# Two fused layers on one core: causal masks added by VectorE inside the maximum, and a unit's last product issued in the next unit

## The reference, cut to what matters

```python
def _causal_attn(q, k, v):
    scale = 1.0 / math.sqrt(q.shape[-1])
    scores = jnp.einsum('bthd,bshd->bhts', q, k) * scale
    t = q.shape[1]
    mask = jnp.tril(jnp.ones((t, t), dtype=bool))
    scores = jnp.where(mask, scores, -jnp.inf)
    attn = jax.nn.softmax(scores, axis=-1)
    return jnp.einsum('bhts,bshd->bthd', attn, v)
...
ctx = _causal_attn(q, k, v)                      # 16 heads of 16 features
conv_out = jax.lax.conv_general_dilated(ctx_c, conv_w, window_strides=(1,), padding=[(1, 1)], ...) + conv_b
q2 = conv_out.transpose(0, 2, 1).reshape(b, s, NUM_HEADS, HEAD_DIM)
ctx2 = _causal_attn(q2, k, v)
out = ctx2.reshape(b, s, d) @ out_w.T + out_b
```

## Time and profile before

| | us |
|---|---|
| median of 3 runs | 2189.26 |
| lowest, highest | 2182.49, 2190.48 |
| the profiled execution, its own time | 2200.97 |
| its span, first to last instruction | 2199.1 |
| last stage (turns 0 to 31 of the second layer), from 1237.7 | 961.4 |
| TensorE busy in the span | 1917.2 (87%) |
| VectorE busy | 1284.2 (58%) |
| ScalarE busy | 905.3 (41%) |
| granted TensorE clock, mean | 0.94 |

### The profile page before, as it was taken

How to read it: one execution, slowest core, us unless ns; L and a number is a source line. 1 busy time by engine, 2 the same in 40 slices (tenths; PEclk the granted TensorE clock), 3 DMA queues, 4 the chain that set the end, 5 groups by cost and what they waited for, 6 DMA issues and landing times.

```text
span 2199.1 us, 32188 instructions
## 1 busy us (share of the span) xinstructions
PE 1917.2 (87%) x11791; PEld 941.1 (43%) x11801; DVE 1284.2 (58%) x2839; ACT 905.3 (41%) x1633; POOL 403.0 (18%) x651
## 2 busy tenths in 40 slices
PE   4888988899858999996589798999999999999987
PEld 2222322323212666664234344545445454545444
DVE  5888778777852333332553665666565656565653
ACT  0354555455533111111244344445444445444444
POOL 3232333123151111111442100000010100000000
PEclk8789989989977999998699899999999999999999
DMA  4445444532413111112104235354543444443440
GB/s 110 102 106 117 110 94 99 95 57 56 87 40 133 32 32 34 30 34 91 38 20 86 45 69 80 60 90 84 83 86 64 87 73 82 81 91 62 73 69 21
DMA packets 131217, 159.55 MB, mean 73 GB/s; under 512 B 22419, under 2 KB 115731, under 8 KB 129014
## 3 DMA queue, kind: packets, MB, share of 16 engines
q1 hardware_dynamic: 126630, 148.18, 34.3%
q0 software_dynamic: 4432, 9.33, 1.5%
HBM read 111.26 MB, written 46.19 MB: 72 GB/s over the span
## 4 chain that ended last, share of the span: by engine, by line
PE 65%; DVE 13%; DMA 7%; ACT 5%; issue 3%; POOL 2%; SPq 2%; another core or an unknown queue 1%; DVEq 0%; POOLq 0%
PE p_PV L659 11%; PE p_S L619 8%; PE p_S L643 8%; PE p_PV L739 6%; DVE t_mx L994 6%; PE p_S L715 5%; PE p_Ma L835 4%; PE p_Ma L589 4%; DMA msd<-t_msp 3%; SPq L1699 2%; PE p_S L646 2%; PE p_S L622 2%; PE p_S L728 2%; PE p_Ma L597 2%; ACT t_spl L1370 2%
## 5 line engine op out<-in xcount | busy, mean ns | idle before, releaser
L1387 ACT ACTIVATE t_R<-p_S 128x512 f32<-128x512 f32 (+1 forms) x1216 | 668.5, 574 | 628.5 <-PE p_S L646 332.6
L994 DVE TENSOR_REDUCE t_mx<-p_S 128x1 f32<-128x512 f32 (+3 forms) x1216 | 750.0, 656 | 219.5 <-PE p_S L622 139.5
L619 PE MATMUL p_S<-t_R 96*128 96x512 bf16 (+3 forms) x1536 | 488.2, 346 | 51.5 <-DVE t_mx L994 31.1
L643 PE MATMUL p_S<-t_R 99*128 99x512 bf16 (+3 forms) x1536 | 487.5, 341 | 43.7 <-ACT t_R L1387 16.6
L659 PE MATMUL p_PV<-t_R 128*17 128x512 f32 (+3 forms) x3072 | 338.4, 514 | 1.7 <-ACT t_R L1387 1.4
L619 PEld LDWEIGHTS p_S<-t_R 96*128 96x128 bf16 x1536 | 151.3, 100 | 397.5 <-DVE t_mx L994 236.9
L643 PEld LDWEIGHTS p_S<-t_R 99*128 99x128 bf16 x1536 | 152.6, 100 | 225.9 <-ACT t_R L1387 96.0
L1588 POOL CAST t_spl<-t_rr 128x512 bf16<-128x512 f32 x80 | 48.9, 611 | 953.3 <-DVE t_rr L958 953.3
L622 PE MATMUL p_S<-t_maskq,t_identb 128*128 128x128 bf16 x1024 | 200.6, 223 | 0.0
L646 PE MATMUL p_S<-t_maskk,t_identb 128*128 128x128 bf16 x1024 | 198.9, 220 | 0.0
L1224 DVE TENSOR_SCALAR t_spl<-p_S,t_B1T 128x128 f32<-128x128 f32 x312 | 84.4, 343 | 135.8 <-PE p_S L728 135.3
(11 more groups left out here) (204 smaller groups left out, 1905.3 us busy)
## 6 DMA issues: line engine op xcount, KB each, us to landing
t_R<-qs SPq DMA_DIRECT2D x288, 128.0 KB, 4.3
t_R<-ks SPq DMA_DIRECT2D x288, 128.0 KB, 4.9
qs<-t_spl SPq DMA_DIRECT2D x48, 384.0 KB, 2.3
t_R<-in_w SPq DMA_DIRECT2D x16, 1024.0 KB, 5.3
ks<-t_spl SPq DMA_DIRECT2D x32, 384.0 KB, 5.7
ysd<-t_cT SPq DMA_DIRECT2D x39, 128.0 KB, 1.7
t_X<-in_x SPq DMA_DIRECT2D x8, 512.0 KB, 3.6
h0d<-t_cT SPq DMA_DIRECT2D x8, 512.0 KB, 2.9
```

The lines of the kernel that those rows point to most:

```text
L619: t = self.nc.tensor.matmul(bank[:, z, :], qa[0:96, h, qb * 128:(qb + 1) * 128], ka[0:96, h, 0:n], start=True, stop=not u.causal)
L643: t = self.nc.tensor.matmul(bank[:, z, :], ka[0:99, h, kb * 128:(kb + 1) * 128], qa[0:99, h, n0:512], start=True, stop=not u.causal)
L994: nc.vector.tensor_reduce(m.mx[:, g, i:i + 4 * len(js) - 3:4], m.S1[k % 3][:, 0:len(js) * n].rearrange("p (j n) -> p j n", j=len(js)), AX. ...
L1387: nc.scalar.activation(m.P[p % 2][:, j0:j0 + per, 0:n], m.s2_bank(k)[:, 0:per * n].rearrange("p (j n) -> p j n", j=per), ACT.Exp, scale=0. ...
```

## The change

1. In `maxp` the mask matmul goes. VectorE's `tensor_reduce` over one to four slices in a bank becomes, for a causal unit, one `tensor_tensor_reduce` for each slice: it adds `maskq`, now 512 columns wide with zeros ahead of the triangle, writes the sum back into the bank, and gives the maximum of the row.
2. The masks are filled with -2^127 by GpSimd at once; VectorE's two multiplications and the semaphore `masks` go.
3. In `expp` a causal unit's last product stays in `self.late` and is issued after the second score step of the next unit, with its `close` behind it (`finish`). A turn still has 26 steps of `expp`.
4. So that the product has its input kept, the exponentials of causal units go into four buffers `P1`, one for each kb; ScalarE waits for the product four back, not two.
5. `pre1` of a kind 2 unit with c = 0 starts four of its steps later (LATE2, steps 8, 10, 12 of the turn in place of 0, 2, 4), `fin1` three of its own (LATE: 9, 12, 15, 18 in place of 0, 3, 6, 9), on all engines.

```diff
 def pre1(self, u):
-        return steps(3 if u.kind == 1 else 2 if u.c else 4)
+        return steps(3 if u.kind == 1 else 2 if u.c else LATE2 + 4)
...
     def expp(self, u):
-        late = None
         for g in range(2):
             for kb in range(4):
...
                     self.scores(u, g, kb, j0, per, n0)
-                    if late is not None and j0 + per >= 2:
-                        self.product(u, *late)
-                        done, late = late, None
-                        if done[1] == 3:
-                            yield
-                            yield from self.close(u, done[0])
+                    if self.late is not None and j0 + per >= 2:
+                        yield from self.finish()
                     yield
-                late = (g, kb)
-        self.product(u, *late)
-        yield
-        yield from self.close(u, 1)
+                self.late = (u, g, kb)
+        if not u.causal or u.n == 47:
+            yield from self.finish()
+
+    def finish(self):
+        (u, g, kb), self.late = self.late, None
+        self.product(u, g, kb)
+        if kb == 3:
+            yield
+            yield from self.close(u, g)
...
 TensorE.maxp
-                                              start=True, stop=not u.causal)
-                    if u.causal:
-                        t = self.nc.tensor.matmul(bank[:, z, n - 128:n], m.identb[:, :], m.maskq[:, :],
-                                                  start=False, stop=True)
+                                              start=True, stop=True)
...
 TensorE.product
-                                      m.P[p % 2][:, j, 0:512 - n0], start=(kb == 0), stop=(kb == 3),
+                                      m.P1[kb][j] if u.causal else m.P[p % 2][:, j, :], start=(kb == 0), stop=(kb == 3),
...
 VectorE.maxp
-                nc.vector.tensor_reduce(
-                    m.mx[:, g, i:i + 4 * len(js) - 3:4],
-                    m.S1[k % 3][:, 0:len(js) * n].rearrange("p (j n) -> p j n", j=len(js)),
-                    AX.X, ALU.max).then_inc(s.s1_read, 1)
+                if u.causal:
+                    e.wait_ge(s.consts, 6)
+                    for z in range(len(js)):
+                        sc = m.S1[k % 3][:, z * n:z * n + n]
+                        x = nc.vector.tensor_tensor_reduce(
+                            out=sc, in0=sc, in1=m.maskq[:, 512 - n:512],
+                            scale=1.0, scalar=NEG, op0=ALU.add, op1=ALU.max,
+                            accum_out=m.mx[:, g, i + 4 * z:i + 4 * z + 1])
+                    x.then_inc(s.s1_read, 1)
+                else:
+                    nc.vector.tensor_reduce(m.mx[:, g, i:i + 1], m.S1[k % 3][:, :], AX.X, ALU.max).then_inc(s.s1_read, 1)
...
 ScalarE.scores
-        if p >= 2:
+        if u.causal and p >= 132:
+            e.wait_ge(s.pv_mm, p - 3)
+        elif u.causal:
+            e.wait_ge(s.x2_base, NB)
+            e.wait_ge(s.p_mm, NB)
+        elif p >= 2:
             e.wait_ge(s.pv_mm, p - 1)
...
 pre1, kind 2, c = 0: TensorE and ScalarE
+            yield from steps(LATE2)
 VectorE, GpSimd and SyncE
-            yield
-            yield
+            yield from steps(LATE2 + 2)
...
 GpSimd.begin
-        g.affine_select(out=m.maskq[:, :], in_=m.maskq[:, :], compare_op=ALU.is_ge, fill=1.0,
-                        **down).then_inc(s.consts, 1)
+        g.affine_select(out=m.maskq[:, 384:512], in_=m.maskq[:, 384:512], compare_op=ALU.is_ge, fill=NEG,
+                        **down).then_inc(s.consts, 1)
```

More of the change, by code:

```diff
@@ L18 @@
 NEG = -(2.0 ** 127)
+LATE2 = 4
+LATE = 3
 QP, KP = (0, 0, 0, 1, 1, 2), (0, 1, 2, 0, 1, 0)
@@ L365, in __init__ @@
         self.c2T = self.xTb
+        self.P1 = [[R2[:, 12288 + 512 * j:12800 + 512 * j] for j in range(4)],
+                   [R2[:, 14336 + 384 * j:14720 + 384 * j] for j in range(4)],
+                   [(R2[:, 15872:16384], R3[:, 512:1024])[j // 2][:, 256 * (j % 2):256 * (j % 2) + 256] for j in range(4)],
+                   [R3[:, 1024 + 128 * j:1152 + 128 * j] for j in range(4)]]
+        self.P1X = [[p.rearrange("p (j n) -> p j n", j=1) for p in self.P1[0]],
+                    [p.rearrange("p (j n) -> p j n", j=1) for p in self.P1[1]],
+                    [R2[:, 15872:16384].rearrange("p (j n) -> p j n", j=2),
+                     R3[:, 512:1024].rearrange("p (j n) -> p j n", j=2)],
+                    [R3[:, 1024:1536].rearrange("p (j n) -> p j n", j=4)]]
     def v_tile(self, u):
@@ L382, in __init__ @@
         self.consts = sem("consts")
-        self.masks = sem("masks")
         self.ones3 = sem("ones3")
@@ L451, in __init__ @@
         self.raw = engine
+        self.late = None
         self.begin()
@@ L507, in pre1 @@
     def pre1(self, u):
-        return steps(3 if u.kind == 1 else 2 if u.c else 4)
+        return steps(3 if u.kind == 1 else 2 if u.c else LATE2 + 4)
     def fin1(self, u):
-        return steps(4) if u.kind == 2 and u.c else none()
+        return steps(LATE + 4) if u.kind == 2 and u.c else none()
     def expp(self, u):
-        late = None
         for g in range(2):
@@ L607, in maxp @@
         e.wait_ge(s.d_f[1][u.buf], 96 * u.fill)
-        if u.causal:
-            e.wait_ge(s.masks, 2)
         for g in range(2):
@@ L849, in fin1 @@
         e, m, s, b = self.e, self.m, self.s, u.b
+        yield from steps(LATE)
         for c in range(2):
@@ L1332, in fin1 @@
         nc, e, m, s, b = self.nc, self.e, self.m, self.s, u.b
-        yield
-        yield
+        yield from steps(LATE + 2)
         for h in range(2):
@@ L1384, in scores @@
         e.wait_ge(s.s2_mm, k + 1)
-        if p >= 2:
+        if u.causal and p >= 132:
[4 more added lines that the diff above has]
+        elif p >= 2:
             e.wait_ge(s.pv_mm, p - 1)
         nc.scalar.activation(
-            m.P[p % 2][:, j0:j0 + per, 0:n], m.s2_bank(k)[:, 0:per * n].rearrange("p (j n) -> p j n", j=per),
+            m.P1X[kb][j0 // per] if u.causal else m.P[p % 2][:, j0:j0 + per, :],
+            m.s2_bank(k)[:, 0:per * n].rearrange("p (j n) -> p j n", j=per),
             ACT.Exp, scale=0.25 if u.causal else 1.0).then_inc(s.s2_exp, 1)
@@ L1502, in begin @@
         down = dict(base=0, pattern=[[-1, 128]], channel_multiplier=1)
-        for t in (m.ident, m.identb, m.maskq, m.maskk):
+        for t in (m.ident, m.maskq, m.identb, m.maskk):
             g.memset(t[:, :], 0.0).then_inc(s.consts, 1)
@@ L1507, in begin @@
                         **down).then_inc(s.consts, 1)
+        g.affine_select(out=m.maskq[:, 384:512], in_=m.maskq[:, 384:512], compare_op=ALU.is_ge, fill=NEG,
+                        **down).then_inc(s.consts, 1)
         g.affine_select(out=m.identb[:, :], in_=m.identb[:, :], compare_op=ALU.not_equal, fill=1.0,
                         **down).then_inc(s.consts, 1)
-        g.affine_select(out=m.maskq[:, :], in_=m.maskq[:, :], compare_op=ALU.is_ge, fill=1.0,
-                        **down).then_inc(s.consts, 1)
-        g.affine_select(out=m.maskk[:, :], in_=m.maskk[:, :], compare_op=ALU.is_ge, fill=1.0, base=0,
+        g.affine_select(out=m.maskk[:, :], in_=m.maskk[:, :], compare_op=ALU.is_ge, fill=NEG, base=0,
                         pattern=[[1, 128]], channel_multiplier=-1).then_inc(s.consts, 1)
@@ L1830, in fin1 @@
         e, m, s, b = self.e, self.m, self.s, u.b
-        yield from steps(4)
+        yield from steps(LATE + 4)
         e.wait_ge(s.out_add, 2 * b + 2)
```

8 lines of the change are left out of this document (2 added, 6 removed).

## The result

The changed kernel takes 2200.96 us in the median of 13 runs (2192.94 to 2208.95); the kernel before took 2185.68 beside it (13 runs, 2179.79 to 2192.97). The ratio is 1.0070, 95% interval 1.0054 to 1.0087: 15 us slower. Forecast were 2208 us, 18.5 over the median of the kernel before. The execution profiled after has a span of 2199.7 us and took 2201.47, near its median; the one of before was 15 us over its own, and lost them between the two attention stages, in code that the change does not touch: the preparation of the second layer's first unit starts at 1048 us there, at 1035 in the changed kernel.

What follows compares the result with a forecast made beforehand. With three banks PE can't run ahead, so VectorE's chain was followed, with late transfers stalling convolution turns. -19.6 + 0 + 15.6 + 9.9 + 13.6 - 1 = +18.5 us on the median 2189.3: 2208 us, range 2150 to 2250.

Steps and rivals of the forecast that it cites:

- the place of the loss: Six convolution turns with output projection: later convolution delays q's write and twelve transfers, each turn 2.6 us longer, +15.6 us.
- Turns 2 and 28: Convolution turns without the output projection: transfers land at 36.4 us, turns 5.3 and 4.6 us longer, +9.9 us.
- the turns with a second convolution: Eight turns (3, 7, ..., 27, 29): 28.3 us forecast, 28.3 in the mean measured before, so 0 change.
- the clock: Eight stalls of over 4 us before PE-heavy convolutions lower the granted clock: 8 x 1.7 = +13.6 us.
- projection turns: Fourteen turns (0, 1, 4, 5, ..., 24, 25): 27.3 us each, 1.4 less, -19.6 us in all.
- A group is then ... 8.78 us, 1.76 more: VectorE's maxima for four heads: 16 instructions, 8.78 us against 7.02 before, 3.5 us more a turn.
- I follow VectorE's chain: Projection turns: PE can't run ahead with three banks, so VectorE's chain sets the turn: 26.8 us, 27.3 with 0.4 added.
- PE has 2.7 us less a turn: PE's queue: 1.86 us a turn from removed mask matmuls and 0.80 from no wait before the last product's transpositions.
- The transfers land in time: Rival: quicker fill or earlier step 12, by 4.6 us together, so no turn stalls: -36 us, 2153 us; chance 0.2.
- The read costs nothing, the stall stays: Rival: the maximum's read is free, 1.3 us off 22 turns, -29 us: net -10, 2179 us; chance 0.17.
- The new maximum is dearer: Rival: its read takes a whole instruction, 2.1 us on 22 turns and 0.8 on eight, +52 us: 2260; chance 0.13.
- PE is the bound and all of its gain is kept: Rival: all 32 turns get 2.7 us shorter, -86 us: 2103 us; chance 0.05.

Runs made afterwards that it cites:

- E2: The kernel before with only the late product, its buffers and the shifts, masks still by matmuls and one maximum a bank: 2217.64 us, ratio 1.0158.
- E4: The changed kernel with SyncE issuing the six transfers of k at the start of the turn, ahead of those of q: 2151.5 us, ratio 0.9858.
- E8: The changed kernel with k's transfers first and the convolution at step 2 instead of 4, last output a step sooner: 2146.7 us, ratio 0.9791.
- E7: The changed kernel with the 1024 mask matmuls put back, adding zeros: 2221.25 us, ratio 1.0156.
- E10: E8 with every causal maximum reading only 128 columns and the exponential's scale 2 to the -14: 2117.5 us, ratio 0.9715.
- E6: E2 (late product alone, masks by matmul) with the transfers of KA issued first: 2168.7 us, ratio 0.9914.
- E9: E8 with the 1024 matmuls put back, adding zeros: 2174.95 us, ratio 0.9962.
- E5: The kernel before with one edit, the transfers that fill KA issued first: 2171.9 us, ratio 0.9915.

## Why the prediction was right, and where its steps were not

**Right: the place of the loss.** The moved convolution carries q's write and twelve transfers with it in SyncE's queue, and they come too late. Written at 21.8 forecast, 21.2 measured; all landed at 36.8, and TensorE released at 36.4 to 37.8; the convolution turn's own work 32.3 and 32.5; the wait "some 4.6" and 3.5 to 4.8 in six turns. E2 and E4 show that this is the cause. One reading was a little off: the "4 us in hand" count to the last packets, and TensorE is released some 1.2 us behind them (31.4 us into turn 6 of the kernel before), so 3 us were in hand. Turns 2 and 28 were put too kindly, because their own work ends at 27.8, and the waits behind them are 9 us, not 7. With its clock the stall's kinds of turn together were forecast at 15.6 + 9.9 + 13.6 = +39.1 us; they are +34.3 (convolution and second-convolution turns 371.8 to 395.5 us, turns 2, 3, 28 and 29 122.4 to 133.0). The sum hides two misses that go against each other: with no stall the turns with a second convolution take 27.0 to 27.1 us (E8), not 28.3, and the clock took more than its term (below). The waits themselves were forecast at 6 x 4.6 + 2 x 6.9 = 41 us, and they are 42.

**Right in kind, a little low: the clock.** +13.6 forecast. All passes of the convolutions in the changed kernel, from the page:

```profile
L845 PE MATMUL p_Ma<-t_cT,t_R 128*128 128x512 f32 x192 | 102.4, 690 | 0.0
```

Before they were 88.1 us, so +14.3; in E8, with no stall left, they are 85.5. The eight turns behind a convolution turn last 278.0 us together in the changed kernel and 216.5 in E8; 42.1 of the 61.5 us between are the waits, so some 19 came behind them, most of it in these passes.

**Right in the sum, wrong in the terms: projection turns.** 27.3 forecast, 27.4 measured; -19.6 and -20.7 us. That they agree is luck. "A group is then ... 8.78 us, 1.76 more": from start to start it is 7.16, and 1.1 more than the 6.1 of before. The prediction took TensorE's price from the starts in the timeline and VectorE's from durations, on both sides. The 60 ns for the read were added to a body of 688, and the read overlaps the next body. Here the Trainium skill ("VectorE: DVE Perf Modes", section "Two Vector instructions with no wait between them") is borne out in that an accumulator output is two instructions, and two rows would have made 859 ns of what takes 650. The turn nevertheless came out because "I follow VectorE's chain" was not the binding chain either: with the prices from the starts it would have given less than the 26.8 us that it gave, and the turn takes 27.4; E7 adds 67 us of VectorE to E2 and costs under 10; E10 takes 5.7 us of VectorE from a turn and gains 0.6. Two errors met, a chain that does not bind and a price too high on it.

**"PE has 2.7 us less a turn": one part came, the other mostly not.** The 0.80 us of the earlier trace rows were gained: no such wait stands at a turn's end any more, as the prediction's sign said, and E2's projection turn is 0.9 us shorter. What is left of the waits for ScalarE's copy is inside the turn. In 1300 to 2120 us, the kernel before, E2 and the changed kernel:

```profile
PE p_Mb L673 <- ACT t_O L1397: 21.5, 27, 0.8
```

```profile
PE p_Mb L687 <- ACT t_O L1413: 8.3, 28, 0.4
```

```profile
PE p_Mb L683 <- ACT t_O L1416: 16.6, 35, 0.7
```

Of the masks' 1.86 us a turn only 0.5 to 0.9 arrive (E6 to E4, E9 to E8). Without them the waits for ScalarE's copy grow, as from the second of these rows to the third.

**Turn 30** fell by 3.6 us, not 1, and turn 31 rose by 1.4. Total: -20.7 + 34.3 - 3.6 + 1.4 = +11.4, the stage's 11.6 but for rounding; forecast +18.5.

**The rivals.** "The transfers land in time" was put at 2153 us; its condition was not met. When E4 makes K's half of them land in time by another order, the kernel takes 2151.5, which is near that price, though two short waits are left and the order helps the kernel before as well (E5). "The read costs nothing, the stall stays", 2179, had the read right; it did not come to pass because the price of VectorE is not what the turns hang on. "The new maximum is dearer", with a whole instruction for its read, is refuted by the starts 0.65 us apart, and "PE is the bound and all of its gain is kept" by the turns, 27.4 us and not 26.0.

## What to carry to other kernels

When a step is moved later, follow it to the last transfer that it releases, and to what stands behind it in the same DMA queue; a stall of 4 us cost its clock besides. Then look whether everything in that queue needs the moved step: here half of the bytes did not, and one line of order turned 0.7% slower into 1.4% faster, and with the shift halved into 2.1%. Work taken off the busiest engine is worth only what the engines it hands over to can follow: test it by putting the work back with no effect (zeros), not by its busy time. And a price that is read from starts on one engine must be read from starts on the other, before and after.

## What was not expected of the hardware

VectorE's fused add and maximum with an accumulator output is shown as a body (718 ns at 512 columns, 323 at 128) and a read of 141 ns, but back to back one takes 0.65 and 0.25 us: the read and the next body start together. A plain maximum from PSUM overlaps the next one as well: 688 ns a row at 512 columns, 0.61 us from start to start. So the fused one is 0.04 us dearer at 512, and four of 128 columns take 1.0 us where one instruction over all four took 0.61. Behind a stall of 3.6 us the granted clock was 0.50 for 3 us, and over turn 29, with its stall above 9 us, 0.87 in the mean.
